# One attention and feed-forward block on one Trainium2 core: the softmax's bias moved from ScalarE to VectorE, with the instruction orders laid anew

## The reference

```python
x = L0_attn_x                                   # (16, 512, 256)
xn = _layernorm(x, axis=-1)
x = x + _L0_attn_ref(xn, wq, wk, wv, wo) + _L0_ffn_ref(xn, k0, k1, k2, s0, s1, s2)

# attention
q = rope(einsum('bim,mhd->bhid', x, wq)); k = rope(einsum('bim,mhd->bhid', x, wk))
v = einsum('bim,mhd->bhid', x, wv)
s = einsum('bhid,bhjd->bhij', q, k) / 128
p = softmax(s - 1e30 * mask, axis=-1)
out = einsum('bhid,hdm->bim', einsum('bhij,bhjd->bhid', p, v), wo)
```

## Time and profile before

| | |
|---|---|
| time, median of 3 runs | 1728.72 us (1728.67 to 1729.3) |
| time of the profiled execution | 1728.13 us |
| its span, first to last instruction | 1726.3 us |
| busy in the span: TensorE, VectorE, ScalarE, GpSimd | 1713.5, 1386.2, 1467.6, 890.4 us |

### The profile page before, as it was taken

One profiled execution on the slowest core, in us unless ns is written; L12 is line 12 of the kernel. 1 busy time (PEld: TensorE's weight loads), 2 busy tenths in 40 slices (PEclk: granted clock), 3 DMA queues, 4 the chain that ended last, 5 costly groups with the idle time before them and its releaser, 6 DMA issues.

```text
span 1726.3 us, 34270 instructions
## 1 busy us (share of the span) xinstructions
PE 1713.5 (99%) x12752; PEld 1202.2 (70%) x12752; DVE 1386.2 (80%) x3374; ACT 1467.6 (85%) x3229; POOL 890.4 (52%) x696
## 2 busy tenths in 40 slices
PE   8999999999999999999999999999999999999999
PEld 4567667677676776767667676676767767677677
DVE  8997887887878878688787877878788787886875
ACT  7898897888979889798897988979789797897984
POOL 7654655354654635556354563555635556354531
PEclk9999999999999999999999999999999999999999
DMA  5234434343434433444434343344433534353343
GB/s 177 56 72 85 93 60 93 68 90 64 76 81 65 98 60 71 86 72 83 68 62 86 74 81 68 68 85 70 92 56 82 79 61 93 58 94 71 62 81 68
DMA packets 454838, 134.08 MB, mean 78 GB/s; under 512 B 434704, under 2 KB 453648, under 8 KB 454672
## 3 DMA queue, kind: packets, MB, share of 16 engines
q1 hardware_dynamic: 454672, 131.90, 40.1%
HBM read 14.94 MB, written 8.39 MB: 14 GB/s over the span
## 4 chain that ended last, share of the span: by engine, by line
PE 95%; ACT 2%; DVE 2%; DMA 1%; SPq 0%; issue 0%; POOL 0%; DVEq 0%; ACTq 0%
PE bank L238 44%; PE bank L699 21%; PE bank L683 12%; PE bank L666 12%; PE bank L710 6%; DMA v<-in_wk 1%; ACT bank L427 1%; DVE pt L514 0%; ACT ph L431 0%; DMA xnat<-in_x 0%; DVE hb L549 0%; DVE ph L585 0%; SPq L282 0%; DVE wq L537 0%; ACT tb L409 0%
## 5 line engine op out<-in xcount | busy, mean ns | idle before, releaser
L351 POOL TENSOR_TENSOR tb<-tb,sin 128x512 f32<-128x512 f32 x256 | 324.7, 1273 | 445.4 <-ACT tb L410 442.7
L354 POOL TENSOR_TENSOR qk<-tb,qk 128x512 f16<-128x512 f32 x256 | 295.7, 1160 | 284.3 <-ACT qk L413 284.1
L699 PE MATMUL bank<-hb,wa 128*128 128x256 f16 x3360 | 391.3, 273 | 0.2 <-DVE ph L585 0.2
L699 PEld LDWEIGHTS bank<-hb,wa 128*128 128x128 fp8e5 x3360 | 327.3, 98 | 53.7 <-DVE ph L585 0.4
L427 ACT ACTIVATE bank<-bank,nm,sc 128x512 f32<-128x512 f32 (+3 forms) x512 | 301.3, 591 | 2.6
L585 DVE SCALAR_TENSOR_TENSOR ph<-bank,rk,ph 128x512 f16<-128x512 f32 (+3 forms) x512 | 254.1, 545 | 23.0 <-ACT ph L431 21.3
L575 DVE CUSTOM_DVE_ANT_0 bank<-bank,mask 128x512 f32<-128x512 f32 (+3 forms) x512 | 238.5, 518 | 20.4 <-PE bank L666 20.1
L557 DVE TENSOR_TENSOR bank<-bank,cos 128x512 f32<-128x512 f32 x256 | 176.7, 697 | 87.3 <-ACT tb L410 87.1
L683 PEld LDWEIGHTS bank<-pt,v 128*128 128x128 f16 x2304 | 203.7, 98 | 41.5 <-DMA pt<-ph 0.8
L431 ACT ACTIVATE ph<-bank,rk 128x512 f16<-128x512 f32 (+3 forms) x512 | 230.1, 541 | 2.4 <-DVE rk L582 1.4
L683 PE MATMUL bank<-pt,v 128*128 128x256 f16 (+1 forms) x2304 | 231.1, 255 | 0.0
(11 more groups left out here) (113 smaller groups left out, 2343.9 us busy)
## 6 DMA issues: line engine op xcount, KB each, us to landing
out<-xnat SPq DMA_DIRECT2D x32, 256.0 KB, 2.2
xnat<-in_x SPq DMA_DIRECT2D x15, 512.0 KB, 3.8
pt<-ph SPq DMA_TRANSPOSE x256, 4.3
o<-in_k SPq DMA_DIRECT2D x1, 1024.0 KB, 7.5
v<-in_wq SPq DMA_DIRECT2D x1, 1024.0 KB, 9.5
v<-in_wk SPq DMA_DIRECT2D x1, 1024.0 KB, 11.3
ph<-in_wv SPq DMA_DIRECT2D x1, 1024.0 KB, 13.5
o<-in_wo SPq DMA_DIRECT2D x1, 1024.0 KB, 10.9
```

Source lines behind the costliest of these rows:

```text
L351: pool.tensor_tensor(tb, tb, SIN[:], ALU.mult).then_inc(s_crossed, 1)
L354: pool.tensor_tensor(QK[:, g % 2, 2 * w + 1, :], TB[:, (2 * g + w) % TRING, :], QK[:, g % 2, 2 * w, :], ALU.subtract).then_inc(s_qk_lo, 1)
L699: mm = pe.matmul(ps[:, 256 * u:256 * u + 256], WA[:, w, k, (2 * j + u) * 128:(2 * j + u) * 128 + 128], HB[:, h, s, k, :], start=first and ...
```

## The change

`row_bias` leaves ScalarE's program and enters VectorE's, as one tensor_scalar of the same 128x4 tile, behind a wait for the head's four maxima (VectorE waits for its own writes). ScalarE's `exponent` still waits for the semaphore `s_bias`. Nothing else is computed otherwise. All five programs are written in another order, and the banks of `ROTATION` are others. The number of TensorE's matmuls, of the DMAs and of every other operation is the same.

```diff
-        def row_bias(act, g):
-            act.activation(NM[:, g % 4, :], MX[:, g % 4, :], ACT.Copy, scale=SC[:, 1:2]).then_inc(s_bias, 1)
...
+        def row_bias(dve, g):
+            dve.tensor_scalar(NM[:, g % 4, :], MX[:, g % 4, :], SC[:, 1:2], None, ALU.mult).then_inc(s_bias, 1)
...
         ROTATION = [
-            [0, 5, 1, 3, 4, 2, 6, 7],
+            [4, 1, 0, 5, 2, 7, 6, 3],
...
-            row_bias(act, 0)
...
             split_w_lo(dve, "v", 1)
             dve.wait_ge(s_crossed, 5)
             dve.wait_ge(s_straight, 5)
-            rotate(dve, 2, 0, BANK[6])
-            h1_first_lo(dve, 2, BANK[0])
+            rotate(dve, 2, 0, BANK[1])
+            dve.wait_ge(s_max, 4)
+            row_bias(dve, 0)
+            h1_first_lo(dve, 3, BANK[6])
```

More of the change, by code:

```diff
@@ L5353, in tensor_program @@
+            scores(pe, 11, 0, BANK[1])
+            pe.wait_ge(s_P_lo, 41)
+            scores(pe, 11, 1, BANK[5])
+            pe.wait_ge(s_P_lo, 43)
+            scores(pe, 11, 2, BANK[2])
+            pe.wait_ge(s_P_lo, 44)
+            v_proj(pe, 1, 1, 3, BANK[0])
+            pe.wait_ge(s_o, 9)
+            qk(pe, 12, 1, BANK[6])
+            pe.wait_ge(s_sum, 2)
+            product(pe, 1, 1, range(8), BANK[3], first=True)
             pe.wait_ge(s_pt[1], 160)
+            pe.wait_ge(s_rot, 25)
@@ L5394, in tensor_program @@
+            pe.wait_ge(s_vp, 15)
+            scores(pe, 13, 2, BANK[6])
+            pe.wait_ge(s_h1, 6)
+            qk(pe, 14, 0, BANK[0])
+            product(pe, 1, 3, range(8), BANK[3])
+            pe.wait_ge(s_pt[1], 192)
             pe.wait_ge(s_rot, 30)
-            scores(pe, 13, 2, BANK[7])
+            values(pe, 11, BANK[5])
             pe.wait_ge(s_o, 11)
-            v_proj(pe, 1, 1, 2, BANK[5])
-            product(pe, 1, 3, range(8), BANK[4])
-            pe.wait_ge(s_pt[1], 192)
@@ L5590, in tensor_program @@
-            pe.wait_ge(s_P_lo, 87)
+            values(pe, 16, BANK[5])
+            pe.wait_ge(s_s5, 3)
+            qk(pe, 21, 1, BANK[4])
+            product(pe, 0, 6, range(8), BANK[7])
+            pe.wait_ge(s_P_lo, 77)
+            qk(pe, 22, 0, BANK[1])
+            pe.wait_ge(s_pt[1], 288)
+            pe.wait_ge(s_P_lo, 80)
+            values(pe, 17, BANK[0])
+            pe.wait_ge(s_o, 17)
+            product(pe, 1, 1, range(8), BANK[5], first=True)
+            pe.wait_ge(s_copy, 8)
@@ new lines, in tensor_program @@
+            product(pe, 1, 6, range(8), BANK[5])
+            product(pe, 1, 2, range(8), BANK[3])
+            pe.wait_ge(s_rot, 45)
+            v_proj(pe, 2, 1, 0, BANK[7])
+            pe.wait_ge(s_h1, 11)
+            v_proj(pe, 2, 1, 3, BANK[6])
+            pe.wait_ge(s_pt[0], 320)
+            pe.wait_ge(s_P_lo, 81)
+            values(pe, 18, BANK[4])
+            pe.wait_ge(s_qk_lo, 45)
+            pe.wait_ge(s_P_lo, 84)
+            scores(pe, 21, 0, BANK[1])
+            pe.wait_ge(s_h1, 12)
@@ new lines, in tensor_program @@
+            scores(pe, 21, 1, BANK[3])
+            pe.wait_ge(s_vp, 21)
+            scores(pe, 21, 2, BANK[7])
+            pe.wait_ge(s_copy, 11)
+            product(pe, 1, 3, range(8), BANK[5])
+            product(pe, 0, 4, range(8), BANK[2])
+            pe.wait_ge(s_vp, 22)
+            qk(pe, 22, 1, BANK[6])
+            pe.wait_ge(s_o, 19)
+            product(pe, 1, 5, range(8), BANK[4], first=True)
+            pe.wait_ge(s_h1, 13)
+            v_proj(pe, 2, 1, 2, BANK[2])
+            pe.wait_ge(s_s5, 4)
@@ new lines, in tensor_program @@
+            product(pe, 1, 1, range(8), BANK[5], first=True)
+            pe.wait_ge(s_copy, 80)
+            product(pe, 0, 3, range(8), BANK[7])
+            product(pe, 0, 2, range(8), BANK[2])
+            pe.wait_ge(s_qk_lo, 234)
+            pe.wait_ge(s_rot, 235)
+            scores(pe, 116, 0, BANK[4])
+            pe.wait_ge(s_o, 114)
+            scores(pe, 116, 1, BANK[0])
+            pe.wait_ge(s_rot, 236)
+            scores(pe, 116, 2, BANK[1])
+            pe.wait_ge(s_h1, 105)
@@ L6129, in tensor_program @@
[L6129 to L6140 removed]
+            pe.wait_ge(s_qk_lo, 237)
@@ L6308, in tensor_program @@
+            pe.wait_ge(s_h1, 114)
+            v_proj(pe, 15, 1, 2, BANK[2])
+            pe.wait_ge(s_pt[1], 1984)
             pe.wait_ge(s_vp, 126)
-            scores(pe, 125, 2, BANK[0])
-            pe.wait_ge(s_h1, 114)
-            v_proj(pe, 15, 1, 1, BANK[3])
-            pe.wait_ge(s_pt[1], 1984)
+            values(pe, 123, BANK[5])
+            product(pe, 0, 3, range(8), BANK[3])
             pe.wait_ge(s_vp, 127)
-            values(pe, 123, BANK[6])
+            product(pe, 1, 5, range(8), BANK[2], first=True)
```

6821 lines of the change are left out of this document (3508 added, 3313 removed), and 26 rows, old and new, of the table ROTATION.

## The result

The changed kernel takes 1752.93 us (median of 4 runs, 1751.26 to 1754.21), the kernel before on the same chip 1728.70 us (1728.59 to 1729.3). The ratio is 1.0139, 95% interval 1.0121 to 1.0156: slower by 24.2 us. The forecast was 1728.4 us, within 1726.2 and 1731.2.

The account below looks back on a forecast made before the run. The prediction took TensorE's matmuls, 106.11 us a loop pass, as the bound. Start -0.3, first heads +0.4 and 100 to 200 us -0.4 summed to -0.3 us: 1728.4 us as a median, range 1726.2 to 1731.2.

Parts of the forecast that it names:

- Onto VectorE: 128 bias tensor_scalars added to VectorE at 0.20 us each, 25.6 us in all, 1.6 us a pass, 0 on the path.
- 0 on the path: The bias work on VectorE, 1.4 to 2.7 us a pass beside some 21 us of idle time, adds nothing.
- The loop's new order: Shortest way, ahead of the scores of a sequence's first head, keeps 0.7 us over, 2.9 at best; put at 0.
- TensorE's work as before, 0 in the loop: In the loop TensorE keeps its matmul work and has no new waits, passes staying 106.1 us; 0.
- a wait in every pass of the loop: Rival: the moved order makes TensorE wait 0.5 us in each of 13 passes, giving 1735 us; chance 0.10.
- The start: Up to the first projection: wq's split ends up to 0.28 us sooner; taken as -0.3 us.
- The slow stretch behind stays: Behind the first projection's wait, 3 us of TensorE work at half clock remain, about 1.5 us lost; no change taken.
- the start is made longer: Rival: VectorE's fullness up to 60 us loses 2 us, 1730.4, or 1731.9 with a second half-clock stretch; chance 0.14.
- The first heads: First exponent at about 54.95 us, a wait behind a p_lo of 0.7 replaces the old 0.3: +0.4 us.
- 100 to 200 us: Biases leave full ScalarE, half of TensorE's 0.9 us of waits returns: -0.4 us, bounds -0.9 and +0.7.
- Off ScalarE: 128 bias instructions, 38.2 us, leave ScalarE, 2.4 us a pass; TensorE never waits for it there, so 0 in the loop.

Follow-up runs that it names:

- a_act: The changed kernel with the bias back on ScalarE, ahead of its head's exponents, orders otherwise as changed: 1744.79 us.
- Experiment 5: The changed kernel with the PSUM-input bias in chosen heads only: first head 1746.80 us, first and third 1740.34, fourth 1750.29, all but the fourth 1738.98.
- experiment 6: The changed kernel with the PSUM-input bias and VectorE's old order at two places of the start: 1738.68 us.
- a_free: The changed kernel with its bias on VectorE as a scalar_tensor_tensor whose bypassed second input is in PSUM: 1739.43 us.
- b_free: The kernel before with only the bias moved to VectorE, behind its head's last maximum, in the form with a PSUM input: 1734.52 us.
- b_dve: The kernel before with only the bias moved to VectorE, as tensor_scalar behind its head's last maximum: 1771.61 us.
- a_free_start: The changed kernel with the PSUM-input bias and, before 28 us, VectorE's old order of first LO part and weight maxima at two places: 1738.68 us.
- a_h3_lock: The changed kernel with the tensor_scalar bias kept in each sequence's fourth head only, the other seven in the PSUM form: 1738.98 us.

## Why the prediction was wrong

**"Onto VectorE ... From below, 170 ns; from above, ScalarE's 298 plus the 34. I take 0.20 us ... 0 on the path."** This step failed. The operation alone does take 0.217 us. It measured 682 ns on the mean and up to 2.04 us, since it waits out a GpSimd instruction under way, and the upper end was no bound at all: it came from ScalarE, where the bias has no such wait (0.28 to 0.33 us in `a_act`, with 82 of the 128 begun beside a GpSimd instruction). "0 on the path" failed with it: two of the eight biases of a pass stand on TensorE's path. The nearest row was the wrong one. In the kernel before, 126 of `inverse`'s 128 tensor_scalars began where GpSimd was idle; that was the order's doing. The trace had another 128x4 tensor_scalar, on the variances, 14 of whose 16 stood beside a GpSimd instruction. Its group in the kernel before:

```profile
L468 DVE TENSOR_SCALAR ve<-mv 128x4 f32<-128x4 f32 x16 | 15.7, 982 | 0.5
```

and the other is the 170 ns of the earlier trace rows. Two means a factor of six apart for one operation on one shape were there to be read, and GpSimd works 52% of the span.

**"The loop's new order ... I put 0."** It failed by the same cause, in another place than I had looked: the scores of the first head, where I found 0.7 us over, aren't waited for in each pass. The waits came behind `rotate` and `difference`, whose readers I had not priced. Experiment 5 shows that the two biases ahead of them make nearly all of it; without these the pass is 106.1 us in the new orders. So "TensorE's work as before, 0 in the loop" was right for the orders in themselves, to 0.1 to 0.2 us in most passes (three in each kernel are 0.2 to 1.3 us longer), and wrong for the instruction that moved.

**The rival "a wait in every pass of the loop"** (0.10) is what happened. It had 0.5 us in 13 passes, 6.5 us; it was 0.8 with a few longer ones, up to 1.8, and 9.7 us of TensorE's idle time from 250 to 1500 us. Its mechanism (the tightest way to the scores) was not the one at work.

**The start, "-0.3 us"**, has the wrong sign: 2.0 us later at the first projection, 3.0 at the first scores (53.1 us for 50.1). The LO part ahead of wk's maximum waited 0.75 us for ScalarE's HI part at 15.84 instead of filling a gap, and the maximum of wo waited 0.73 for its data. But experiment 6 takes the first away for nothing: the old order waits there for data instead. The end of the split is set by GpSimd's row, which I had not looked at. The 2.49 us of the k split, which the prediction took from its row without a cause, are of the same kind: that split ended at 33.74 us, 0.55 behind a GpSimd instruction. **"The slow stretch behind stays"**: it doubled, to 6.8 us at half clock, behind a wait of 4.2 instead of 3.2 us; the length of the wait alone doesn't explain it, since five other kernels with the wait of 4.2 have 3.4 us there. The rival "the start is made longer" (0.14) described this, with 2 us and 1.5 for the clock.

**The first heads, "+0.4 us", and 100 to 200 us, "-0.4 us".** The first `exponent` started at 58.34 us, not at 54.95. The wait behind a `p_lo` that made the +0.4 did not come; TensorE idles 0.9 us from 60 to 100 us behind other waits, where it had none. From 100 to 200 us it idles 1.6 us more than before where 0.4 less was forecast. The largest wait there is the one given as the upper bound, a LO part of a projection that comes late: 1.26 us instead of at most 0.7. In `a_free` it is 1.10 and in `a_act` it is there too, so it belongs to the new orders and not to the bias.

**"Off ScalarE ... worth 0 in the loop"** was right to 0.1 us: in the new orders the bias on ScalarE gives passes of 106.3 us, in the PSUM form on VectorE 106.2.

**What stays open.** `a_free` loses 10.7 us with 211 ns a bias. Against the kernel before, TensorE is idle 6.8 us more in it (1.7 in the first 60 us, 2.3 from 60 to 250, 2.0 in the loop up to 1500) and busy 4.8 us more. Of the 4.8 the clock explains at most 3.4: it was at half for 3.4 us before and for 10.2 us, in two stretches, in `a_free`. The first projection's 2.6 us are the split's step. `b_free` reaches the split late too, at 29.86, with nothing moved ahead of it (it waited 1.15 us for the data of wq), so that part is not the order's alone. What makes the idle time from 60 to 250 us and in the loop was not separated: moved instructions and the waits of `inverse` are both candidates. None of the ten kernels beats the one before.

## What to carry to other kernels

Before small work goes to VectorE, look at what GpSimd does at that moment: take the duration from rows of the same operation beside a busy GpSimd, and if there is none, the upper bound is its own time plus GpSimd's longest instruction, and more where GpSimd's instructions follow each other without a gap: here 2.04 us beside one and 3.50 beside three, for a 0.2 us step. Where the wait can't be avoided by the place, give the instruction one SBUF input and let the second be in PSUM; that was worth 13.5 us in one order and 37 in the other. Then look which instruction takes the wait over; here it was in part `inverse`, with 12 us. What such a wait costs goes by what is queued right behind it: 2.04 us ahead of slack cost nothing where it stood alone, 1.23 us ahead of a bank that TensorE wanted cost 6.

## What the runs showed of the hardware

- A tensor_scalar with four columns took 0.21 us alone, up to 2.04 us beside one GpSimd instruction, and 3.50 us in `b_dve` beside three in a row; one with two columns (`dg`) took up to 1.67. Its record includes the wait, so the page shows a busy engine and the list of waits puts TensorE's idle time down to the instruction behind it.
- scalar_tensor_tensor has no wait with a PSUM second input (at most 0.22 us, all 128), and the tensor_scalar's wait with a second input in SBUF (678 ns, though it is bypassed).
- Of the biases with their inputs in SBUF, 14 of the 19 that began with 0.25 us or more of GpSimd's tensor_scalar `xT` to go did not wait; all 450 that began so beside its tensor_tensors did.
- Where the bias waits, its end follows GpSimd's by 0.02 to 0.03 us.
- In `a_free` the granted clock was 0.50, 1.2 GHz, for 3.4 us from 12.7 and for 6.8 us from 33.2 us, behind a wait of 4.2 us; the kernel before had 3.4 us from 31.0, behind one of 3.2, and `b_free` none at the start with a wait of the same 3.2. With the wait of 4.2 us it was 6.8 us in four kernels (the changed one, `a_free`, `a_free_start`, `a_h3_lock`) and 3.4 in five. I have no account of that.
